# A decoder layer on one core: the experts' second layer with weights and data exchanged, and new instruction orders

## The reference

```python
x = x + attn(layernorm(x))     # down to 64 channels, rmsnorm, two window attentions (windows of 10 and of 20
                               # tokens, 8 heads of 4 channels each, relative bias, shifted, softmax), project up,
                               # add, rmsnorm, gelu feed-forward 128 -> 256 -> 128, add
x = x + xattn(ctx, layernorm(x))   # k = v = ctx @ Wq.T, causal softmax(q k^T / sqrt(128)) v, one head
h = layernorm(x)               # router: softmax over 8 experts, the two largest keep their probability
shared = gelu(h @ sw1 + sb1) @ sw2 + sb2
mixed  = sum_e w[:, e] * (gelu(h @ rw1[e] + rb1[e]) @ rw2[e] + rb2[e])
x = x + shared + mixed
```

## Time and profile before

| | us |
|---|---|
| median of three runs | 178.4 (176.14 to 179.72) |
| the profiled execution, time | 176.86 |
| its span, first to last instruction | 174.6 |
| PE / DVE / ACT / POOL busy | 159.2 / 115.3 / 84.2 / 32.8 |
| granted TensorE clock, mean | 0.966 |

### The profile page before, as it was taken

One profiled execution on the slowest core, in us unless ns is written; L12 is line 12 of the kernel. 1 busy time (PEld: TensorE's weight loads), 2 busy tenths in 40 slices (PEclk: granted clock), 3 DMA queues, 4 the chain that ended last, 5 costly groups with the idle time before them and its releaser, 6 DMA issues.

```text
span 174.6 us, 3350 instructions
## 1 busy us (share of the span) xinstructions
PE 159.2 (91%) x1276; PEld 125.7 (72%) x1276; DVE 115.3 (66%) x284; ACT 84.2 (48%) x154; POOL 32.8 (19%) x56
## 2 busy tenths in 40 slices
PE   7889999999979758798899999999999999999991
PEld 2647665676958345557778797777989989889990
DVE  6786669999498989867753465558663755413352
ACT  2004920071166237286477949494372783453500
POOL 3569950000000340023405002010022000000000
PEclk9969999995699999999999999999999999999998
DMA  5998000000000000000000000000000010000002
GB/s 154 366 315 356 6 4 0 0 4 4 0 0 0 4 0 2 0 0 0 0 6 0 0 4 0 0 0 0 0 4 0 4 46 18 0 0 4 0 0 60
DMA packets 2876, 5.93 MB, mean 34 GB/s; under 512 B 354, under 2 KB 1996, under 8 KB 2605
## 3 DMA queue, kind: packets, MB, share of 16 engines
q1 hardware_dynamic: 2544, 5.44, 9.3%
q10 hardware_dynamic: 316, 0.29, 0.5%
HBM read 5.20 MB, written 0.52 MB: 33 GB/s over the span
## 4 chain that ended last, share of the span: by engine, by line
PE 76%; DVE 12%; POOL 4%; issue 4%; ACT 3%; DVEq 0%; POOLq 0%; ACTq 0%
PE ps L1275 71%; DVE prod L953 3%; PE ps L1539 2%; POOL rstd L457 2%; DVE prod L960 1%; POOL xs L494 1%; PE ps L1333 1%; ACT xcT L639 1%; DVE stat L974 1%; POOL rstd L455 1%; DVE xcT L995 1%; ACT v_sb L601 1%; DVE prod L931 1%; DVE prod L921 1%; DVE vn L978 1%
## 5 line engine op out<-in xcount | busy, mean ns | idle before, releaser
L1275 PEld LDWEIGHTS ps<-moe_w_sb,hid 128*128 128x128 f32 x288 | 34.3, 192 | 1.9 <-issue 1.0
L1275 PE MATMUL ps<-moe_w_sb,hid 128*128 128x128 f32 x288 | 34.6, 275 | 0.0
L720 ACT ACTIVATE hid<-ps,consts_sb 128x512 f32<-128x512 f32 x36 | 24.4, 687 | 18.1 <-PE ps L1275 18.0
L1132 DVE SCALAR_TENSOR_TENSOR acc<-ps,wts,acc 128x128 f32<-128x128 f32 x64 | 18.0, 343 | 16.4 <-PE ps L1275 16.3
L1275 PE MATMUL ps<-xf_hi,w_hi 128*128 128x512 f32 x36 | 16.0, 446 | 0.0
L1275 PE MATMUL ps<-prod,half_ident 128*128 128x400 f32 x36 | 14.0, 511 | 1.5 <-DVE prod L931 1.3
L1275 PE MATMUL ps<-xf_lo,w_hi 128*128 128x512 f32 x36 | 14.2, 394 | 0.0
L1275 PE MATMUL ps<-xf_hi,w_lo 128*128 128x512 f32 x36 | 14.2, 393 | 0.0
L455 POOL TENSOR_SCALAR rstd<-mv 128x1 f32<-128x1 f32 (+3 forms) x12 | 3.0, 248 | 57.4 <-DVE mv L1061 30.6
L457 POOL TENSOR_TENSOR rstd<-rstd,minus_half 128x1 f32<-128x1 f32 (+3 forms) x16 | 12.8, 798 | 1.3
L921 DVE TENSOR_TENSOR prod<-qkv 128x400 f32<-128x400 f32 (+1 forms) x16 | 11.5, 782 | 1.0 <-ACT qkv L573 1.0
(11 more groups left out here) (157 smaller groups left out, 278.2 us busy)
## 6 DMA issues: line engine op xcount, KB each, us to landing
moe_w_sb<-in_moe_w SPq DMA_DIRECT2D x2, 1152.0 KB, 10.0
pr<-in_ctx SPq DMA_DIRECT2D x1, 576.0 KB, 6.4
out<-acc SPq DMA_DIRECT2D x8, 64.0 KB, 1.7
late_sb<-in_late SPq DMA_DIRECT2D x1, 404.0 KB, 10.4
ffn_hids<-in_bias SPq DMA_DIRECT2D x1, 369.7 KB
x_sb<-in_x SPq DMA_DIRECT2D x1, 320.0 KB, 3.5
acc<-in_x_cols SPq DMA_DIRECT2D x1, 320.0 KB, 4.4
x_sb<-in_x SPq DMA_DIRECT2D x1, 192.0 KB, 4.9
```

The source lines that it names most:

```text
L720: act.activation(hid[:, k % DEEP, c, :], ps[:, c, :], ACT.Gelu, bias=cols_sb[:, i:i + 1]).then_inc(moe_h_ready, 1)
L1132: dve.scalar_tensor_tensor(acc[:, g, :], ps[:, slot_bank(n), t * D:(t + 1) * D], wts[h][:, t, e:e + 1], acc[:, g, :], ALU.mult, ALU.add).t ...
L1275: return pe.matmul(dst, lhs, rhs, start=start, stop=stop)
```

## The change

**Second layer.** `output(h, e, c)` now holds the weight `w2` in the array and streams 512 tokens of hidden values, in three fp32r products like `hidden`; all nine experts of a half add up in one PSUM bank (2 for half 0, 3 for half 1), channels by tokens. Since a token's weight can no longer be applied to a result lying tokens by channels, DVE multiplies the hidden values by it (`moe_gate`, in place, 128x512, experts 1 to 8). The weights must stand in every partition for that: they are turned (`weight_rows`, now 27 rows), copied (`wT_copy`), stored to DRAM by SP and read back to all 128 partitions, one 256 KB load for each expert and half. ACT copies the gated hidden values to fp32r (`moe_high`), DVE forms the rest (`moe_low`). `w2` is split once (`w2_high` on ACT, three `w2_low` on DVE). The biases are one fp32r product with 27 rows into the same bank. At the end of a half ACT copies the bank out (`y_copy`), TensorE turns it back to tokens (`y_tokens`), and DVE adds it to `acc` (`x3_tiles`). `moe_add`, `shared_add` and `bias_add` are gone, and half 0's output rows are stored only at the end.

**Other parts.** Half 0's feed-forward up to `x1_columns` and the POOL steps with it run in two pieces of two tiles (`PIECES`). `PAIRED` holds all four branch halves, `QUARTERED` is empty. First-layer results of half 1 rotate through four banks instead of two (`Z_BANKS`). Branch 1 comes before branch 0 in the window attention; branch 0 of half 1 from `window_scores` on is moved behind half 0's `x1_moments`. All five queues have new orders. Buffers are placed anew so that the new tiles fit.

```diff
-PAIRED = ((0, 1), (1, 1))
+Z_BANKS = ((0, 1), (0, 1, 4, 5))
+Y_BANKS = ((6, 6, 6, 6), (2, 6, 7, 4))
+PAIRED = ((0, 0), (1, 0), (0, 1), (1, 1))
-QUARTERED = ((1, 0), (1, 1))
+QUARTERED = ()
+PIECES = (((0, 2), (2, 4)), ((0, 4),))
...
         # SP
+            for h in range(HALVES):
+                sp.wait_ge(wT_ready, h + 1)
+                sp.dma_start(gate_rows[:, h * CH:(h + 1) * CH], wT[:]).then_inc(gates_stored, 16)
+                sp.wait_ge(gates_stored, 16 * (h + 1))
...
+                for e in range(1, EX):
+                    if h and e > E // 2:
+                        sp.wait_ge(gated, gated_count(0, e - E // 2))
+                    sp.dma_start(gate(h, e), gate_rows[e:e + 1, h * CH:(h + 1) * CH].broadcast_to([P, CH])).then_inc(ld_gate[h][e - 1], 16)
...
         # ACT
+            def w2_high():
+                act.wait_ge(ld_moe, 16)
...
+                act.activation(w2_hi[:], moe_w2_sb[:], ACT.Copy).then_inc(w2_high_ready, 1)
+                if q >= DEEP * NC:
+                    act.wait_ge(low_ready, q - DEEP * NC + 1)      # in moe_gelu
+            def moe_high(h, e, c):
+                q = (h * EX + e) * NC + c
+                if e:
+                    act.wait_ge(gated, gated_count(h, e - 1) + c + 1)
...
+                act.activation(part_at(high, q), hidden_at(q), ACT.Copy).then_inc(high_ready, 1)
+            def y_copy(h, a, z):
+                act.wait_ge(moe_ps, (h + 1) * EX * NC)
+                act.activation(x1T[h][:, a * P:z * P], ps[:, 2 + h, a * P:z * P], ACT.Copy).then_inc(y_ready, z - a)
...
         # DVE
+            def moe_gate(h, e, c):
+                dve.wait_ge(ld_gate[h][e - 1], 16)
+                dve.wait_ge(moe_h_ready, q + 1)
+                dve.tensor_tensor(hidden_at(q), hidden_at(q), gate(h, e), ALU.mult).then_inc(gated, 1)
+            def moe_low(h, e, c):
+                dve.wait_ge(high_ready, q + 1)
...
+                dve.tensor_tensor(part_at(low, q), hidden_at(q), part_at(high, q).bitcast(F32),
+                                  ALU.subtract).then_inc(low_ready, 1)
+            def x3_tiles(h, a, z):
+                dve.wait_ge(y_tok_ps, h * TH + z)
+                for t in range(a, z):
+                    dve.tensor_tensor(acc[:, g, :], ps[:, Y_BANKS[h][t], t * D:(t + 1) * D], acc[:, g, :],
+                                      ALU.add).then_inc(x3_ready, 1)
...
         # PE
+            def output(h, e, c):
+                y = ps[:, 2 + h, :]
+                pe.wait_ge(high_ready, q + 1)
+                mm(y, w2_hi[:, e, c, :], part_at(high, q), start=(e == 0 and c == 0), stop=False)
+                mm(y, w2_lo[:, e, c, :], part_at(high, q), start=False, stop=False)
+                pe.wait_ge(low_ready, q + 1)
+                last = mm(y, w2_hi[:, e, c, :], part_at(low, q), start=False, stop=(e == EX - 1 and c == NC - 1))
+            def y_tokens(h, a, z):
+                pe.wait_ge(y_ready, h * TH + z)
...
+                else:
+                    pe.wait_ge(x3_ready, TH)
```

More of the change, by code:

```diff
@@ L226, in decoder_layer @@
         ld_moe = sem("ld_moe")
+        ld_b2 = sem("ld_b2")
+        gates_stored = sem("gates_stored")
+        ld_gate = [[sem(f"ld_gate_{h}_{e}") for e in range(E)] for h in range(HALVES)]
         stored = sem("stored")
@@ L1248, in _ @@
             x2_norm(5)
+            moe_low(0, 4, 0)
+            moe_gate(0, 5, 0)
+            x2_norm(6)
+            b2_low()
+            moe_gate(0, 5, 1)
             x2_tile(7)
             x2_moments(7)
-            x2_norm(6)
+            moe_gate(0, 6, 0)
             x2_norm(7)
-            moe_add(0, 6)
+            moe_low(0, 4, 1)
+            moe_low(0, 5, 0)
+            moe_low(0, 5, 1)
+            router_logits(1)
+            router(1)
             xf_low(1, 0)
             xf_low(1, 1)
-            moe_add(0, 7)
@@ new lines, in _ @@
+            moe_gate(0, 8, 0)
+            moe_gate(0, 8, 1)
+            moe_low(0, 7, 0)
+            moe_low(0, 7, 1)
+            moe_low(0, 8, 0)
+            moe_low(0, 8, 1)
+            moe_low(1, 0, 0)
+            moe_low(1, 0, 1)
+            moe_gate(1, 1, 0)
+            moe_gate(1, 1, 1)
+            moe_gate(1, 2, 0)
+            moe_gate(1, 2, 1)
+            moe_gate(1, 3, 0)
+            moe_low(1, 1, 0)
+            moe_low(1, 1, 1)
+            moe_low(1, 2, 0)
+            moe_low(1, 2, 1)
@@ new lines, in _ @@
+            moe_low(1, 3, 0)
+            moe_gate(1, 3, 1)
+            moe_gate(1, 4, 0)
+            moe_gate(1, 4, 1)
+            moe_gate(1, 5, 0)
+            moe_gate(1, 5, 1)
+            moe_low(1, 3, 1)
+            moe_low(1, 4, 0)
+            moe_gate(1, 6, 0)
+            moe_gate(1, 6, 1)
+            moe_gate(1, 7, 0)
+            moe_low(1, 4, 1)
+            moe_low(1, 5, 0)
+            moe_low(1, 5, 1)
+            moe_low(1, 6, 0)
+            moe_low(1, 6, 1)
+            moe_low(1, 7, 0)
@@ L1272, in _ @@
+            moe_gate(1, 7, 1)
+            moe_gate(1, 8, 0)
+            moe_gate(1, 8, 1)
+            moe_low(1, 7, 1)
+            moe_low(1, 8, 0)
+            moe_low(1, 8, 1)
+            x3_tiles(0, 0, 4)
+            x3_tiles(1, 0, 1)
+            x3_tiles(1, 1, 2)
+            x3_tiles(1, 2, 3)
+            x3_tiles(1, 3, 4)
         @block.tensor
@@ L1808, in _ @@
-            output(1, 7)
-            output(1, 8)
+            y_tokens(0, 0, 4)
+            output(1, 5, 0)
+            output(1, 5, 1)
+            output(1, 6, 0)
+            output(1, 6, 1)
+            output(1, 7, 0)
+            output(1, 7, 1)
+            output(1, 8, 0)
+            output(1, 8, 1)
+            y_tokens(1, 0, 1)
+            y_tokens(1, 1, 2)
+            y_tokens(1, 2, 3)
+            y_tokens(1, 3, 4)
 def kernel(**inputs):
```

922 lines of the change are left out of this document (561 added, 361 removed).

## The result

The changed kernel takes **171.66 us** (median of 4 runs, 171.31 to 172.15), the kernel before, beside it, 177.76 (176.14 to 179.72, 4 runs): a ratio of 0.969, 95% interval 0.961 to 0.977. The forecast was 172.5, in a range of 166 to 180. The profiled execution took 172.15 us with a span of 170.0 (before: 176.86, span 174.6).

What follows compares the result with a forecast made beforehand. TensorE was taken to bound the experts, DVE the front: first `hidden` 88.2 plus TensorE's 73.1 gives 161.3, plus 4 for turns 165.3, plus tail 5.0 a span of 170.3, plus 2.26 around it 172.5 us; range 166 to 180.

Steps and rivals of the forecast that it cites:

- TensorE's floor: Experts' stage: 82.1 us less 7.2 for `output` and 1.8 for bias products, so 73.1 us.
- DVE: 3 us too much work: DVE from the end of `x2_norm(3)`: 73.9 us needed, including 44.9 for gates and lows and 3 of waits.
- The turns: Experts: at some 12 turns from gates to lows DVE may wait for ACT's copy, a third of a microsecond each, 4 us.
- the two rivals built on the turn: Experts: turns cost 0.5 to 1 us each, 177.5 us (chance 0.24); or DVE becomes the bound, 184.5 us (0.13).
- the one of no waits: Rival: both queues interlock without waits; the 4 us and most of the front's 7 vanish, 163 to 168 us (chance 0.13).
- The front: Up to half 0's `x2_norm(3)`: start 18.2, DVE work 60.3, waits 7, ending at 85.5 us against 87.03.
- the loads ahead of `qkv_copy`: Front, ACT: `bias_split` and `w1_high` wait for loads; a first `hidden` later than 90 by them was a sign of wrong.
- The clock: Front: the slow-clock stretch of TensorE was counted at nothing, as DVE is the bound there.
- `w2_high` at nothing: ACT before the experts: 2.1 us costed at nothing under DVE's last moments; without cover, up to 2.1 later first `hidden`.
- The tail: After TensorE's last `output`: 5.0 us against 3.8, with `y_tokens(1)` waiting for `x3_tiles(0)` and a copy and turn added.
- The loads: Gates through DRAM: 3 us per 256 KB load, covered by queued DVE work; up to 6 us uncovered near the upper end.
- the rule cited ahead: GpSimd contends with DVE's two-SBUF-input instructions; half 1's four normalisation powers stretch 0.5 each, 2 us if on the path, 174.5.

Runs made afterwards that it cites:

- two_products: The changed kernel without the product of the high hidden part with w2's low part, 36 of 108 second-layer products: 168.91 us.
- gates_small: The changed kernel with half 1's 16 gate multiplications done on one column instead of 512: 172.08 us.
- xi_first: The changed kernel with `xi_rows` issued ahead of the five dummy products on TensorE: 171.89 us.
- squares_order: The changed kernel with `xf_high(0, 1)` ahead of `xp_squares(1, 0)` on ScalarE and `hidden(0, 1, 0)` ahead of `h_columns(1, 0)` on TensorE: 172.73 us.
- again: The changed kernel run once more, unedited, as reference for the other kernels on its chip: 171.69 us.
- front_before: The changed kernel's experts' stage behind the orders of the kernel before, with pairs only in half 1 and half 0's feed-forward in one piece: 177.93 us.
- both_small: The changed kernel without those 36 second-layer products and with the gates of both halves on one column: 166.89 us.
- front_before2: front_before with `w2_high` and `b2_high` moved ahead of `window_exp(1, 1)` and `xp_squares(1, 0)` behind `xf_high(0, 1)`: 176.64 us, 0.997 of the kernel before.
- whole: The changed kernel with half 0's feed-forward in one piece of four tiles, orders otherwise as in the change: 172.74 us.
- held: The changed kernel with two more dummy products in each long row of narrow products, in `qkv_rows(1, 0)` and `qkv_rows(1, 1)`: 171.81 us.

## Why the prediction was right, step by step

**TensorE's floor: right in mechanism, 1.1 too low.** The 108 products stand at 0.23, and two_products and gates_small show that this engine sets the stage. But TensorE is busy 74.2 of its 75.2 us, against a floor of 73.1. The sum took the changeover's 0.09 out of every expert; yet the first product behind one of another form still takes longer (the two groups that come first have means of 432 and 418 ns, the others 392). That this is the 1.1 is likely, not shown.

**DVE: 3 us too much work.** Gates and lows are busy for 43.4 us together, 0.64 each (0.66 and 44.9 forecast; their means of 0.68 contain the overlap). From the end of `x2_norm(3)` to the last low at 163.0 DVE works 67.9 us, 70.9 forecast, and is idle 7.5, 3 forecast. It is second, by 3 us (two_products), not by 2.

**The turns: the step that failed.** 4 us were given to waits between the two queues. The trace shows 1.0 us of idle TensorE in the whole stage, and none of it at a turn: it lies from 90 to 102 us, where `h_columns` and `hT` of half 1 are late (0.73 and 0.23 named on TensorE's timeline). From 102 on there is none, and DVE waited 0.3 us for `moe_high` in all. So the term was 4 us and measured 0. The order gates far enough ahead that a copy of 0.62 is done before its low. This kills the two rivals built on the turn; the one of no waits named the mechanism, but its 163 to 168 also wanted the front's 7 us.

**The front: 2 us too good.** `x2_norm(3)` ended at 87.50, not 85.5. DVE's work was 60.33 (forecast 60.3) and its waits 68.14 - 60.33 = 7.8 (forecast 7); the rest is the first product, 19.36 against 18.2. I had looked for the danger in the loads ahead of `qkv_copy`, and overlooked the dummies ahead of `xi_rows`. xi_first shows that this 1.2 isn't the bound either: freed, it goes into a wait that the profile doesn't name. From `x2_norm(3)` to the first `hidden` it is 2.8 us, 2.7 forecast, but not by the squares alone. They take ScalarE 1.3 us and hold up the first `hidden` by 0.7 (1.0 forecast); about 0.5 comes from `to_tokens(1)` ahead of the last `xf_columns`, a move that was put at nothing. squares_order shows no gain without the squares' 0.7: TensorE then waits 0.24 and 0.86 us inside the first `hidden` calls. A first `hidden` later than 90 was named as a sign of being wrong, by the loads ahead of `qkv_copy`; it came at 90.27 here and 89.61 in again, and the copy had waited 2.0 us for TensorE, not for a load.

**The clock: wrongly counted at nothing.** "As DVE is its bound" does not hold: DVE waited 3.5 us behind products at half clock (2.1 to 3.5 in the six executions with this front). What the front would be worth at full clock no run shows.

**`w2_high` at nothing: right, because of its place.** It ran from 84.32 to 86.44 under DVE's last moments. In front_before it lay under TensorE's wait for `xcT` and cost nothing to be seen either, so the 2.1 named for a place without cover was never measured.

**The tail** was 4.5, forecast 5.0. **The loads** of the gates, 4.0 to 5.7 us each (3 forecast), never held a gate: DVE's idle time ahead of the gates is 0.1 us.

**POOL.** Half 1's four normalisations: the groups of the kernel before, then of the changed kernel:

```profile
L457 POOL TENSOR_TENSOR rstd<-rstd,minus_half 128x1 f32<-128x1 f32 x4 | 2.2, 547 | 0.3
...
L455 POOL TENSOR_SCALAR rstd<-mv 128x1 f32<-128x1 f32 x4 | 0.8, 200 | 23.2 <-DVE mv L1061 23.2
```

```profile
L550 POOL TENSOR_TENSOR rstd<-rstd,minus_half 128x1 f32<-128x1 f32 x4 | 3.2, 791 | 0.3
...
L548 POOL TENSOR_SCALAR rstd<-mv 128x1 f32<-128x1 f32 x4 | 1.9, 463 | 18.7 <-DVE mv L1258 18.7
```

They grew by 0.51 us each, beside half 0's gates and lows. gates_small, which shortens only half 1's gates, has 0.791 and 0.461; both_small, where half 0's are one column too, has 0.710 and 0.281. By the rule cited ahead (the Trainium skill, "GPSIMD Engine Reference", section "Key points"), the trace agrees. But it costs no time, since TensorE waits for none of them.

So the mechanism was right, and the closeness of the number is luck, by parts that offset: the front 2.1 and TensorE's own work 1.1 worse, the waits in the stage 3.0 and the tail 0.5 better. The forecast also took the front for a small gain; front_before and front_before2 show that with the old one nothing is left of the stage's gain.

**What stays open.** How the 5 us between front_before2 and the changed kernel divide between orders, the added pairs of values and the clock was not separated: `whole` bounds the pieces at about 1, and the pairing of half 0 alone wasn't tried. Nor is it known what the wait inside `qkv_rows` is that took xi_first's gain. What makes the clock fall is not settled: the first fall came at 19.9 us in the first profile and at 18.9 in again's, behind a row of narrow products, but near the start of that row in held (16.2) and whole (14.2); in squares_order it fell behind three waits of 0.2 to 0.9 us.

## What to carry to other kernels

Price a stage by the engine that never waits in it, and ask of the second engine only whether its order runs far enough ahead; then per-step handovers cost nothing, as here. A microsecond won ahead of a chain over three engines is won only if that chain is what was waiting: check the next two waits, not the one removed. Work that stands right ahead of a late start need not be its cause: 2.3 us of splittings did, and lay under another engine's wait. And take a second trace of the same program before pricing a wait: the 3.5 us that two experiments set out to remove was 2.1 in the next execution, with nothing changed.

## What the runs showed of the hardware

- TensorE's granted clock fell at different places in two executions of one program. In the first it fell at 19.9 us, 1.2 behind a row of 160 products of 33x24, with TensorE busy 6.5 of the 7.9 us before; again at 36.9, in the second such row, with TensorE busy all of the 4.9 us before. In again's it fell at 18.9 and 39.3, 0.6 and 1.3 behind these rows. `keys` took 2.88 us in the first and 3.62 in again's.
- POOL's `xn_tiles` took 1.89 us a tile beside DVE's window products, 1.21 where the kernel before had it earlier.
- A 128x512 copy on ScalarE from SBUF to SBUF with rounding takes 0.62 us, a gelu of the same size from PSUM 0.68.
- How far a kernel's runs spread differed between orders: 171.3 to 172.3 in eight runs of the changed kernel, 171.5 to 175.0 in four of squares_order, 175.9 to 182.6 for the kernel before. Why wasn't tested.
